# First attention: scores as three products on 64 rows, all engines ordered by pairs of units

## The chip, the cores and the metric

One core of one Trainium2 chip. The metric is the device time of a whole execution in microseconds. The median of three runs of the kernel before is 1353.7 us.

## The reference, cut to what matters

The program is a stack of four blocks on x of 4 x 512 tokens of 256 numbers, each added to x: an attention over a context, a layer of experts, a banded attention over the same context, a second layer of experts. The change touches the first attention alone:

```python
Qh = (queries @ Wq).reshape(n, t, HEADS, D_K)      # queries: layernorm(x), 16 heads of 64
Kh = (keys @ Wk).reshape(n, t, HEADS, D_K)         # keys, values: ctx
Vh = (values @ Wv).reshape(n, t, HEADS, D_V)
energy = jnp.einsum('nqhd,nkhd->nhqk', Qh, Kh) * scale
energy = jnp.where(mask == 0, jnp.asarray(-1e+20, dtype=energy.dtype), energy)
attention = jax.nn.softmax(energy, axis=-1)
heads_out = jnp.einsum('nhqk,nkhd->nqhd', attention, Vh)
return heads_out.reshape(n, t, HEADS * D_V) @ Wo
```

## The kernel before

Numbers that have to be exact are held as a sum of two fp16 tensors, hi and lo (`Split`). A product of two such numbers is three matmuls (`three_products`, L195 to L199): hi hi, hi lo, lo hi.

`phase_attention0` (L235) runs over 4 batches and in each over 8 pairs of heads, 32 groups g in all. A group has 8 units u: two heads a, four tiles qt of 128 queries. Before the change the four tiles of head 0 come first, then those of head 1. A unit goes through five steps. TensorE makes the scores, 128 x 512, into the PSUM bank `sc` (`score`, L419). VectorE adds the mask and takes the maximum (`maximum`, L532, operation L542). ScalarE takes the exponent (`exponent`, L486). TensorE transposes the result in four pieces into `et` (`turn`, L430), ScalarE writes the hi part (`turned_part`, L480) and VectorE the lo part (L516), and TensorE multiplies by v in 12 matmuls of 65 columns (`attend`, L438), the 65th column being the sum of the exponents. After four units of a head VectorE divides (`normalize`, L520).

Each engine runs an order written out by hand. TensorE in turn u does the scores of unit u, the transposes of unit u - 3, the product with v of unit u - 5 (`TURN_LAG`, `ATTEND_LAG`), and then a side job, if there is one. Side jobs (`side_work`, L202) are bound to the unit j within the group: at j = 0 and 1 the projections k and q of the next group, at j = 4 a part of v of the next batch (not in the last batch), at j = 5 in four groups of the second to fourth batch the output projection w of a query tile of the batch before, at j = 7 the transposes t of the outputs of the group before. All side jobs write one of two PSUM banks `pj` in turn, so a job waits until the one two before it has been copied out (`open_group`, L359). The copy is made by ScalarE into `raw` (`copy`, L473), in its turn after that of the job, behind `turned_part` and `exponent` of that turn; for w it is an addition by VectorE. GpSimd then splits `raw` into hi and lo (`split`, L312, operations L333 and L335). `ORDER0` lists all side jobs in order, `GROUP0` and `COPY0` give each its number.

The scores have a contraction over 64 numbers, half of the array's rows. Before the change hi and lo of q are stacked on 128 rows, and k hi twice and k lo twice, by DMA from `nat` (`stack`, L281): so one matmul gives hi hi + lo hi and a second gives hi lo + lo lo (L427, L428). SP's queue issues these eight transfers a group, and behind them the loads of the mask for the next batch.

Of the kernel before, what the change touches and what calls it, by code (L numbers as in the profile page):

```python
# [16 lines left out]
P = 128  # L17
B, S, D = 4, 512, 256
NT = B * S // P
QT = S // P  # L20
# [214 lines left out]
def phase_attention0(nc, sem, T, dram):  # L235
    NBUF = 4
    NRAW = 3
    TURN_LAG, ATTEND_LAG = 3, 5
    with ExitStack() as ctx:
        sb, ps = make_tensors(nc, ctx)  # L240
        v = [Split(sb, f"v{i}", [P, QT, HEADS, VP]) for i in range(2)]
        raw = [sb(f"raw{i}", [P, 512]) for i in range(NRAW)]
        nat = {"q": sb("nat_q", [P, 2, S], F16), "k": sb("nat_k", [P, 2, S], F16)}
        qq = [sb(f"qq{i}", [P, 2, S], F16) for i in range(2)]
        kk = [sb(f"kk{i}", [P, 2, 2, S], F16) for i in range(2)]
        o = [sb(f"o{i}", [P, QT, P]) for i in range(2)]
        o_t = [Split(sb, f"o_t{i}", [P, CT, S]) for i in range(2)]
        masked = [sb(f"masked{i}", [P, S]) for i in range(NBUF)]
# [13 lines left out]
        stacked = [sem(f"stacked{a}") for a in range(2)]  # L262
# [4 lines left out]
        STACKED = 4 * 16  # L267

        def v_part(part, n):
            return part[:, n // 2, (n % 2) * 8:(n % 2 + 1) * 8, 0:DK]  # L270

        with nc.Block() as block:

            @block.sync
            def _(sp):
                def load_mask(n):
                    if n >= 2:
                        sp.wait_ge(bias_ok, n - 1)
                    sp.dma_start(mask_raw[n % 2][:], dram["mask"][n // QT, (n % QT) * P:(n % QT + 1) * P, :]).then_inc(mask_in[n % 2], 16)

                def stack(g):  # L281
                    i = g % 2
                    sp.wait_ge(split_done, COPY0["k", g] + 1)
                    if g >= 2:
                        sp.wait_ge(scores, (g - 1) * UNITS)
                    for a in range(2):
                        for half in range(2):
                            sp.dma_start(kk[i][half * DK:(half + 1) * DK, a, :, :], nat["k"][a * DK:(a + 1) * DK, :, :]).then_inc(stacked[a], 16)
                    sp.wait_ge(split_done, COPY0["q", g] + 1)
                    for a in range(2):  # L290
                        for half in range(2):
                            sp.dma_start(qq[i][half * DK:(half + 1) * DK, a, :], nat["q"][a * DK:(a + 1) * DK, half, :]).then_inc(stacked[a], 16)

                load_mask(0)
                load_mask(1)
                stack(0)
                load_mask(2)
                load_mask(3)
                for g in range(PAIRS0 - 1):
                    stack(g + 1)  # L300
                    if g // PAIRS + 1 < B and g % PAIRS < QT:
                        load_mask((g // PAIRS + 1) * QT + g % PAIRS)

            @block.gpsimd
            def _(pool):
# [52 lines left out]
            def _(pe):  # L358
# [57 lines left out]
                    else:  # L416
                        project_out(what)

                def score(u):  # L419
                    g, j = u // UNITS, u % UNITS  # L420
                    a, qt = j // QT, j % QT
                    if j % QT == 0:
                        pe.wait_ge(stacked[a], STACKED * (g + 1))
                    if u >= 2:
                        pe.wait_ge(masked_ok, u - 1)
                    stat = qq[g % 2][:, a, qt * P:(qt + 1) * P]
                    pe.matmul(sc[j % 2][:], stat, kk[g % 2][:, a, 0, :], start=True, stop=False)  # L427
                    pe.matmul(sc[j % 2][:], stat, kk[g % 2][:, a, 1, :], start=False, stop=True).then_inc(scores, 1)  # L428

                def turn(u):  # L430
                    pe.wait_ge(exp_ok, u + 1)
# [5 lines left out]

                def attend(u):  # L438
                    g, j = u // UNITS, u % UNITS
                    b, a, head = g // PAIRS, j // QT, (g % PAIRS) * 2 + j // QT  # L440
                    if j % QT == 0 and g >= 1:
                        pe.wait_ge(normed, 2 * g - 1 + a)
                    if u % (PAIRS * UNITS) == 0:
                        pe.wait_ge(split_done, COPY0["v", (b, V_GROUPS - 1)] + 1)
                    pe.wait_ge(turned_lo, u + 1)
                    for kt in range(QT):
                        vv = (v[b % 2].hi[:, kt, head, 0:DK + 1], v[b % 2].lo[:, kt, head, 0:DK + 1])
                        mm = three_products(pe, ob[a][:, j % QT, 0:DK + 1], (e_t[u % NBUF].hi[:, kt, :], e_t[u % NBUF].lo[:, kt, :]), vv, kt == 0, kt == QT - 1)
                    mm.then_inc(pv_done, 1)

                project(("k", 0), T.wk0, T.ctx_t)
# [2 lines left out]
                    project_v(("v", (0, n)))  # L454
                pe.wait_ge(v_const, 4)
                units = PAIRS0 * UNITS
                for u in range(units + ATTEND_LAG):
                    if u < units:
                        score(u)
                    if 0 <= u - TURN_LAG < units:  # L460
                        turn(u - TURN_LAG)
                    if u >= ATTEND_LAG:
                        attend(u - ATTEND_LAG)
                    what = side_work(u // UNITS, u % UNITS) if u < units else None
                    if what is not None:
                        do_side_work(what)
# [5 lines left out]
            def _(act):  # L472
# [22 lines left out]
                for n in range(V_GROUPS):  # L495
                    copy(("v", (0, n)))
                units = PAIRS0 * UNITS
                for u in range(units + TURN_LAG):
                    if u >= TURN_LAG:
                        turned_part(u - TURN_LAG)  # L500
                    if u < units:
                        exponent(u)
                    what = side_work((u - 1) // UNITS, (u - 1) % UNITS) if 1 <= u <= units else None
                    if what in COPY0:
                        copy(what)
                copy(("t", PAIRS0 - 1))

            @block.vector
            def _(dve):
# [22 lines left out]
                def maximum(u):  # L532
# [9 lines left out]
                    nc.vector.tensor_tensor_reduce(masked[u % NBUF][:], sc[j % 2][:], mask_bias[g // PAIRS % 2][:, j % QT, :],  # L542
                                                   -SCALE0, 3e38, ALU.add, ALU.min, neg_max[:, g % 2, j:j + 1]).then_inc(masked_ok, 1)

                units = PAIRS0 * UNITS
                for u in range(units + TURN_LAG):
                    if u < units:
                        maximum(u)
                    if u >= TURN_LAG:
                        turned_part(u - TURN_LAG)  # L550
                    if u < units:
                        what = side_work((u - 1) // UNITS, (u - 1) % UNITS) if u >= 1 else None
                        if what in ADD0:
                            add_out(what)
# [1431 lines left out]
```

## Time and profile before

| what | value |
|---|---|
| median of three runs | 1353.7 us (1353.0 to 1359.14) |
| the profiled execution, its own time | 1355.88 us |
| its span | 1354.1 us |
| TensorE busy | 1105.1 us, 82% |
| VectorE busy | 773.4 us, 57% |
| ScalarE busy | 631.1 us, 47% |
| GpSimd busy | 530.1 us, 39% |
| mean granted TensorE clock | 0.908 |

The first attention fills the stretch from about 50 to 577 us. Shares over the span mix stages with different limits, so the stage is read by itself. In the timelines the first column is the start and the second the length, both in us; at the end of a line stands in brackets how long the engine sat idle and what released it. A TensorE matmul is shown with its whole length through the array, so lengths overlap and the distance of two starts is what a matmul takes of the engine. PE is TensorE, DVE VectorE, ACT ScalarE, POOL GpSimd.

### The profile page before, as it was taken

To read this page: it belongs to the slowest core of one execution; us is meant where nothing else is said; L and a number is where in the kernel's file an instruction comes from. 1 tells how busy PE (TensorE), PEld (TensorE's weight loads), DVE (VectorE), ACT (ScalarE), POOL (GpSimd) and SP (SyncE) were. 2 spreads that over 40 slices of the span, in tenths; PEclk is the share of its full clock that TensorE was granted. 3 is DMA by queue.
4 is the path that set the end of the run, shared out by engine and by line. 5 is a ranking of instruction groups with operands and counts; after the bars stand their busy time and mean duration, and the time that the engine had idled before them with its cause. 6 is when DMAs were issued, how large, how long until landed. Compare 5 with 4: busy or idle time off the path is not lost. (4 is left out here: it accounts for less than half of the span.)

```text
span 1354.1 us, 29409 instructions
## 1 busy us (share of the span) xinstructions
PE 1105.1 (82%) x10704; PEld 842.2 (62%) x10705; DVE 773.4 (57%) x2164; ACT 631.1 (47%) x1191; POOL 530.1 (39%) x517
## 2 busy tenths in 40 slices
PE   2399999999999999763999545487899951799996
PEld 1156777777777777562788422355666641688886
DVE  7267787777778778466111062276687651355553
ACT  3277786678668777321222022044455520333331
POOL 2565645545544433190454340588700004011112
PEclk8699999999999999855899859799999975899998
DMA  6222222222222222052365425465422051121110
GB/s 248 54 58 70 53 67 70 57 49 70 68 56 55 48 63 58 1 204 85 107 187 154 89 63 186 127 163 164 127 50 50 18 149 63 33 32 28 26 24 10
DMA packets 80271, 111.08 MB, mean 82 GB/s; under 512 B 11600, under 2 KB 58448, under 8 KB 79760
## 3 DMA queue, kind: packets, MB, share of 16 engines
q1 hardware_dynamic: 69680, 88.30, 22.7%
q0 software_dynamic: 10464, 21.07, 6.7%
q8 instruction: 81, 1.33, 0.4%
q14 instruction: 46, 0.38, 0.1%
HBM read 59.93 MB, written 24.77 MB: 63 GB/s over the span
## 5 line engine op out<-in xcount | busy, mean ns | idle before, releaser
L542 DVE CUSTOM_DVE_ANT_0 masked<-sc,mask_bias 128x512 f32<-128x512 f32 x256 | 175.4, 686 | 58.6 <-issue 39.7
L518 DVE TENSOR_TENSOR e_t_lo<-et,e_t_hi 128x512 f16<-128x512 f32 x256 | 176.6, 690 | 49.8 <-ACT e_t_hi L484 47.4
L491 ACT ACTIVATE e<-masked,neg_max 128x512 f32<-128x512 f32 x256 | 184.0, 719 | 26.6 <-DVE neg_max L542 26.1
L484 ACT ACTIVATE e_t_hi<-et 128x512 f16<-128x512 f32 x256 | 152.0, 594 | 89.5 <-PE et L435 89.0
L435 PEld LDWEIGHTS et<-ident,e 128*128 128x128 f32 x1024 | 125.7, 141 | 54.1 <-ACT e L491 6.1
L435 PE MATMUL et<-ident,e 128*128 128x128 f32 x1024 | 154.2, 273 | 1.4 <-ACT e L491 0.7
L1348 ACT ACTIVATE d_e<-d_st 128x384 f32<-128x384 f32 (+1 forms) x192 | 97.8, 528 | 117.9 <-PE d_st L1433 102.7
L197 PE MATMUL ob<-v_hi,e_t_hi 128*128 128x65 f16 x1024 | 119.1, 193 | 0.6 <-DVE e_t_lo L518 0.6
L198 PE MATMUL ob<-v_lo,e_t_hi 128*128 128x65 f16 x1024 | 119.2, 193 | 0.0
L199 PE MATMUL ob<-v_hi,e_t_lo 128*128 128x65 f16 x1024 | 118.5, 193 | 0.0
L427 PE MATMUL sc<-kk,qq 128*128 128x512 f16 x256 | 97.0, 379 | 6.1 <-DMA qq<-nat_q 5.9
L197 PE MATMUL h_hb<-h_xt_hi,experts_hi 128*128 128x256 f16 x352 | 96.9, 275 | 4.3 <-DVE h_xt_lo L1814 3.9
L1785 POOL DMA_INDIRECT out<-h_res,h_token x22 | 34.3, 1557 | 167.0 <-DVE h_res L1837 161.3
L428 PE MATMUL sc<-kk,qq 128*128 128x512 f16 x256 | 96.9, 379 | 0.0
L198 PE MATMUL h_hb<-h_xt_lo,experts_hi 128*128 128x256 f16 x352 | 96.9, 275 | 0.0
L199 PE MATMUL h_hb<-h_xt_hi,experts_lo 128*128 128x256 f16 x352 | 96.8, 275 | 0.0
L198 PEld LDWEIGHTS ob<-v_lo,e_t_hi 128*128 128x128 f16 x1024 | 94.6, 97 | 2.9
L197 PEld LDWEIGHTS ob<-v_hi,e_t_hi 128*128 128x128 f16 x1024 | 95.7, 97 | 0.8 <-DVE e_t_lo L518 0.7
L199 PEld LDWEIGHTS ob<-v_hi,e_t_lo 128*128 128x128 f16 x1024 | 94.7, 97 | 0.0
L1428 PE MATMUL d_wk<-d_k,d_q 128*128 128x384 f16 (+1 forms) x256 | 71.7, 308 | 23.3 <-DMA d_q<-d_k 20.2
L478 ACT ACTIVATE raw<-pj 128x512 f32<-128x512 f32 x128 | 75.0, 586 | 32.2 <-POOL v_lo L335 16.0
L1360 DVE TENSOR_REDUCE d_mx<-d_wk 128x1 f32<-128x384 f32 x128 | 66.9, 553 | 40.0 <-PE d_wk L1433 33.5
(322 smaller groups left out, 2872.9 us busy)
## 6 DMA issues: line engine op xcount, KB each, us to landing
kk<-nat_k SPq DMA_DIRECT2D x128, 128.0 KB, 2.3
raw<-in_fc SPq DMA_DIRECT2D x16, 1024.0 KB, 6.4
qq<-nat_q SPq DMA_DIRECT2D x128, 64.0 KB, 2.0
mask_raw<-in_mask SPq DMA_DIRECT2D x16, 256.0 KB, 2.9
scratch_stack<-c_qk_hi SPq DMA_DIRECT2D x32, 128.0 KB
scratch_stack<-c_qk_lo SPq DMA_DIRECT2D x32, 128.0 KB
d_expert_raw<-in_gate_w POOLq DMA_DIRECT2D x8, 512.0 KB, 4.3
d_expert_raw<-in_up_w POOLq DMA_DIRECT2D x8, 512.0 KB, 4.0
```

What stands on the lines that cost most here:

```text
L197: pe.matmul(out, stat[0], mov[0], start=first, stop=False)
L198: pe.matmul(out, stat[0], mov[1], start=False, stop=False)
L199: return pe.matmul(out, stat[1], mov[0], start=False, stop=last)
L427: pe.matmul(sc[j % 2][:], stat, kk[g % 2][:, a, 0, :], start=True, stop=False)
L428: pe.matmul(sc[j % 2][:], stat, kk[g % 2][:, a, 1, :], start=False, stop=True).then_inc(scores, 1)
L435: mm = pe.transpose(et[u % 2][:, kt, :], e[u % NBUF][:, kt * P:(kt + 1) * P], T.ident[:])
L478: nc.scalar.activation(raw[n % NRAW][:], pj[GROUP0[what] % 2][:], ACT.Copy).then_inc(copied, 1)
L484: nc.scalar.activation(e_t[u % NBUF].hi[:], et[u % 2][:], ACT.Copy).then_inc(turned_hi, 1)
L491: nc.scalar.activation(e[u % NBUF][:], masked[u % NBUF][:], ACT.Exp, bias=neg_max[:, g % 2, j:j + 1], scale=-1.0).then_inc(exp_ok, 1)
L518: nc.vector.tensor_tensor(e_t[u % NBUF].lo[:], et[u % 2][:], e_t[u % NBUF].hi[:], ALU.subtract).then_inc(turned_lo, 1)
L542: nc.vector.tensor_tensor_reduce(masked[u % NBUF][:], sc[j % 2][:], mask_bias[g // PAIRS % 2][:, j % QT, :], -SCALE0, 3e38, ALU.add, ALU.m ...
L1348: nc.scalar.activation(part(e[m % EBUF][:, 2 * half + i // 3, :, :], i % 3), src, ACT.Exp, scale=SCALE1).then_inc(exp_ok, 1)
```

## The change

Both heads' score of one query tile become one step of TensorE, `score_both`: six matmuls in three rounds, in each round one for head 0 on rows 0 to 63 of the array and one for head 1 on rows 64 to 127, into the two banks `sc`. Their operands are hi and lo of q and k as GpSimd splits them, double buffered; the stacking DMAs, `nat`, `qq`, `kk` and the semaphores for them are gone, and SP's queue holds only mask loads. Units are now ordered by query tile first, head second, and each engine goes on by two units in a turn: TensorE does both scores, both transposes of the pair two back, the side job of the first unit, both products with v of the pair three back, the side job of the second unit. ScalarE does two `turned_part`, two `exponent`, and then the copies of the side jobs of the pair before. VectorE does two maxima, two lo parts, additions, and once in a group both normalizations. The lags become 4 and 6.

```diff
-    TURN_LAG, ATTEND_LAG = 3, 5
+    TURN_LAG, ATTEND_LAG = 4, 6
...
-        nat = {"q": sb("nat_q", [P, 2, S], F16), "k": sb("nat_k", [P, 2, S], F16)}
-        qq = [sb(f"qq{i}", [P, 2, S], F16) for i in range(2)]
-        kk = [sb(f"kk{i}", [P, 2, 2, S], F16) for i in range(2)]
+        heads = {kind: [Split(sb, f"{kind}_heads{i}", [P, S]) for i in range(2)] for kind in ("q", "k")}
...
-                for g in range(PAIRS0 - 1):
-                    stack(g + 1)
-                    if g // PAIRS + 1 < B and g % PAIRS < QT:
-                        load_mask((g // PAIRS + 1) * QT + g % PAIRS)
+                for n in range(NT):
+                    load_mask(n)
...
-                        if at >= 1:
-                            pool.wait_ge(stacked[0], STACKED * at)
-                            pool.wait_ge(stacked[1], STACKED * at)
-                        hi, lo = nat[kind][:, 0, :], nat[kind][:, 1, :]
+                        if at >= 2:
+                            pool.wait_ge(scores, (at - 1) * UNITS)
+                        hi, lo = heads[kind][at % 2].hi[:], heads[kind][at % 2].lo[:]
...
-                def score(u):
...
+                def score_both(u):
+                    g, qt = u // UNITS, u % UNITS // 2
+                    if u % UNITS == 0:
+                        pe.wait_ge(split_done, COPY0["q", g] + 1)
                     if u >= 2:
-                        pe.wait_ge(masked_ok, u - 1)
...
+                        pe.wait_ge(masked_ok, u)
+                    q, k = heads["q"][g % 2], heads["k"][g % 2]
+                    for n, (stat, mov) in enumerate(((q.hi, k.hi), (q.hi, k.lo), (q.lo, k.hi))):
+                        for a in range(2):
+                            rows = slice(a * DK, (a + 1) * DK)
+                            mm = pe.matmul(sc[a][:], stat[rows, qt * P:(qt + 1) * P], mov[rows, :], start=(n == 0), stop=(n == 2))
+                            if n == 2:
+                                mm.then_inc(scores, 1)
...
-                for u in range(units + ATTEND_LAG):
+                for u in range(0, units + ATTEND_LAG, 2):
+                    side = [side_work((u + i) // UNITS, (u + i) % UNITS) if u < units else None for i in range(2)]
                     if u < units:
-                        score(u)
+                        score_both(u)
                     if 0 <= u - TURN_LAG < units:
                         turn(u - TURN_LAG)
+                        turn(u - TURN_LAG + 1)
+                    if side[0] is not None:
+                        do_side_work(side[0])
                     if u >= ATTEND_LAG:
                         attend(u - ATTEND_LAG)
...
+                        attend(u - ATTEND_LAG + 1)
+                    if side[1] is not None:
+                        do_side_work(side[1])
...
-                for u in range(units + TURN_LAG):
+                for u in range(0, units + TURN_LAG, 2):
+                    side = [side_work((u - 2 + i) // UNITS, (u - 2 + i) % UNITS) if 2 <= u <= units else None for i in range(2)]
                     if u >= TURN_LAG:
                         turned_part(u - TURN_LAG)
+                        turned_part(u - TURN_LAG + 1)
                     if u < units:
                         exponent(u)
...
+                        exponent(u + 1)
+                    for what in side:
+                        if what in COPY0:
+                            copy(what)
...
-                    dve.wait_ge(pv_done, g * UNITS + (a + 1) * QT)
+                    dve.wait_ge(pv_done, (g + 1) * UNITS - 1 + a)
...
-                        if u % UNITS == 1 and u >= UNITS:
+                        if u % UNITS == 4 and u >= UNITS:
                             normalize(u // UNITS - 1, 0)
-                        if u % UNITS == 5 and u >= UNITS:
                             normalize(u // UNITS - 1, 1)
```

## Rows read from the trace of the kernel before

**Rows 1.** The page's 40 slices: busy tenths of TensorE.

```profile
PE   2399999999999999763999545487899951799996
```

**Rows 2.** Windows: start, end, length; busy PE, PEld, DVE, ACT, POOL; clock, DMA share, GB/s.

```profile
117.00:549.00 432.00, 428.95 (x5002) 319.93 (x5001) 334.46 (x1043) 326.56 (x565) 206.05 (x224) 1.00 0.24 59
```

**Rows 3.** Waits of 30 to 110 us and of 110 to 549: total, times, longest.

```profile
PE sc L427 <- DMA qq<-nat_q: 2.2, 1, 2.2
...
PE sc L427 <- DMA qq<-nat_q: 3.7, 4, 1.2
```

**Rows 4.** TensorE's timeline, 402.5 to 405.1: start, length, then what ran.

```profile
402.47 0.19 PE L197 MATMUL ob<-v_hi,e_t_hi 128*128 128x65 f16 x1
...
402.83 0.38 PE L197 MATMUL pj<-wv_hi,ctx_t_hi 128*128 128x512 f16 x1
...
404.13 0.38 PE L427 MATMUL sc<-kk,qq 128*128 128x512 f16 x1
404.35 0.38 PE L428 MATMUL sc<-kk,qq 128*128 128x512 f16 x1
404.56 0.60 PE L435 MATMUL et<-ident,e 128*128 128x128 f32 x4
405.00 0.19 PE L197 MATMUL ob<-v_hi,e_t_hi 128*128 128x65 f16 x1
```

**Rows 5.** GpSimd's timeline, 399 to 414: splits of k.

```profile
399.45 0.61 POOL L333 CAST nat_k<-raw 128x512 f16<-128x512 f32 x1 [0.57 <-ACT raw L478]
400.14 1.16 POOL L335 TENSOR_TENSOR nat_k<-raw,nat_k 128x512 f16<-128x512 f32 x1
...
413.63 0.61 POOL L333 CAST nat_k<-raw 128x512 f16<-128x512 f32 x1 [0.21 <-ACT raw L478]
```

**Rows 6.** Groups by line and form: count, busy us, mean ns.

```profile
L427 PE MATMUL sc<-kk,qq 128*128 128x512 f16 x256 | 97.0, 379 | 6.1 <-DMA qq<-nat_q 5.9 <-DVE neg_max L542 0.2
...
L1472 PE MATMUL d_ob<-d_e,v 128*17 128x384 f32 x256 | 23.6, 486 | 0.0
```

**Rows 7.** TensorE's timeline, 908.7 to 911.6, second attention.

```profile
908.79 0.38 PE L1467 MATMUL d_ob<-ident,band 128*128 128x512 bf16 x1
909.10 2.35 PE L1472 MATMUL d_ob<-d_e,v 128*17 128x256 f32 x32
911.38 0.28 PE L1428 MATMUL d_wk<-d_k,d_q 128*128 128x256 f16 x1
```

**Rows 8.** ScalarE's timeline, 404.5 to 407.5.

```profile
405.20 0.60 ACT L484 ACTIVATE e_t_hi<-et 128x512 f16<-128x512 f32 x1 [0.70 <-PE et L435]
405.69 0.71 ACT L491 ACTIVATE e<-masked,neg_max 128x512 f32<-128x512 f32 x1
406.30 0.59 ACT L478 ACTIVATE raw<-pj 128x512 f32<-128x512 f32 x1
406.78 0.60 ACT L484 ACTIVATE e_t_hi<-et 128x512 f16<-128x512 f32 x1
```

**Rows 9.** The timeline of all engines, 66.3 to 67.2.

```profile
66.37 0.60 ACT L478 ACTIVATE raw<-pj 128x512 f32<-128x512 f32 x1 [11.40 <-POOL v_lo L335]
...
67.03 0.61 PE L197 MATMUL pj<-wv_hi,ctx_t_hi 128*128 128x512 f16 x1 [10.53 <-ACT raw L478]
```

**Rows 10.** VectorE's timeline, 404.5 to 407.5.

```profile
404.77 0.69 DVE L542 CUSTOM_DVE_ANT_0 masked<-sc,mask_bias 128x512 f32<-128x512 f32 x1 [0.42 <-issue]
...
405.83 0.69 DVE L518 TENSOR_TENSOR e_t_lo<-et,e_t_hi 128x512 f16<-128x512 f32 x1 [0.36 <-ACT e_t_hi L484]
406.43 0.17 DVE L527 RECIPROCAL rden<-ob 128x4 f32<-128x4 f32 x1
...
406.99 0.69 DVE L542 CUSTOM_DVE_ANT_0 masked<-sc,mask_bias 128x512 f32<-128x512 f32 x1
```

**Rows 11.** The timeline of all engines, 555.0 to 555.9.

```profile
555.05 0.69 DVE L518 TENSOR_TENSOR e_t_lo<-et,e_t_hi 128x512 f16<-128x512 f32 x1 [0.47 <-ACT e_t_hi L484]
...
555.79 0.20 PE L197 MATMUL ob<-v_hi,e_t_hi 128*128 128x65 f16 x1 [0.62 <-DVE e_t_lo L518]
```

More of the change, by code:

```diff
@@ L261, in phase_attention0 @@
         pj_full, copied, added, split_hi, split_done, v_const = (sem(n) for n in ("pj_full", "copied", "added", "split_hi", "split_done", "v_const"))
-        stacked = [sem(f"stacked{a}") for a in range(2)]
         scores, masked_ok, exp_ok = sem("scores"), sem("masked_ok"), sem("exp_ok")
@@ L266, in phase_attention0 @@
         mask_in, bias_ok = [sem(f"mask_in{i}") for i in range(2)], sem("bias_ok")
-        STACKED = 4 * 16
         def v_part(part, n):
@@ L279, in load_mask @@
                     sp.dma_start(mask_raw[n % 2][:], dram["mask"][n // QT, (n % QT) * P:(n % QT + 1) * P, :]).then_inc(mask_in[n % 2], 16)
[L281 to L298, printed above, removed]
-                for g in range(PAIRS0 - 1):
-                    stack(g + 1)
-                    if g // PAIRS + 1 < B and g % PAIRS < QT:
-                        load_mask((g // PAIRS + 1) * QT + g % PAIRS)
+                for n in range(NT):
+                    load_mask(n)
             @block.gpsimd
@@ L417, in do_side_work @@
                         project_out(what)
-                def score(u):
[L420 to L423, printed above, removed]
-                    if u >= 2:
-                        pe.wait_ge(masked_ok, u - 1)
-                    stat = qq[g % 2][:, a, qt * P:(qt + 1) * P]
-                    pe.matmul(sc[j % 2][:], stat, kk[g % 2][:, a, 0, :], start=True, stop=False)
-                    pe.matmul(sc[j % 2][:], stat, kk[g % 2][:, a, 1, :], start=False, stop=True).then_inc(scores, 1)
+                def score_both(u):
+                    g, qt = u // UNITS, u % UNITS // 2
+                    if u % UNITS == 0:
+                        pe.wait_ge(split_done, COPY0["q", g] + 1)
+                    if u >= 2:
+                        pe.wait_ge(masked_ok, u)
[6 more added lines that the diff above has]
+                                mm.then_inc(scores, 1)
                 def turn(u):
@@ L439, in attend @@
                     g, j = u // UNITS, u % UNITS
-                    b, a, head = g // PAIRS, j // QT, (g % PAIRS) * 2 + j // QT
-                    if j % QT == 0 and g >= 1:
+                    b, a, qt, head = g // PAIRS, j % 2, j // 2, (g % PAIRS) * 2 + j % 2
+                    if qt == 0 and g >= 1:
                         pe.wait_ge(normed, 2 * g - 1 + a)
@@ L447, in attend @@
                         vv = (v[b % 2].hi[:, kt, head, 0:DK + 1], v[b % 2].lo[:, kt, head, 0:DK + 1])
-                        mm = three_products(pe, ob[a][:, j % QT, 0:DK + 1], (e_t[u % NBUF].hi[:, kt, :], e_t[u % NBUF].lo[:, kt, :]), vv, kt == 0, kt == QT - 1)
+                        mm = three_products(pe, ob[a][:, qt, 0:DK + 1], (e_t[u % NBUF].hi[:, kt, :], e_t[u % NBUF].lo[:, kt, :]), vv, kt == 0, kt == QT - 1)
                     mm.then_inc(pv_done, 1)
@@ L456, in _ @@
                 units = PAIRS0 * UNITS
-                for u in range(units + ATTEND_LAG):
+                for u in range(0, units + ATTEND_LAG, 2):
+                    side = [side_work((u + i) // UNITS, (u + i) % UNITS) if u < units else None for i in range(2)]
                     if u < units:
-                        score(u)
+                        score_both(u)
                     if 0 <= u - TURN_LAG < units:
                         turn(u - TURN_LAG)
+                        turn(u - TURN_LAG + 1)
+                    if side[0] is not None:
+                        do_side_work(side[0])
                     if u >= ATTEND_LAG:
                         attend(u - ATTEND_LAG)
-                    what = side_work(u // UNITS, u % UNITS) if u < units else None
-                    if what is not None:
-                        do_side_work(what)
+                        attend(u - ATTEND_LAG + 1)
+                    if side[1] is not None:
+                        do_side_work(side[1])
                 turn_out(("t", PAIRS0 - 1))
@@ L497, in _ @@
                 units = PAIRS0 * UNITS
-                for u in range(units + TURN_LAG):
+                for u in range(0, units + TURN_LAG, 2):
+                    side = [side_work((u - 2 + i) // UNITS, (u - 2 + i) % UNITS) if 2 <= u <= units else None for i in range(2)]
                     if u >= TURN_LAG:
                         turned_part(u - TURN_LAG)
+                        turned_part(u - TURN_LAG + 1)
                     if u < units:
                         exponent(u)
-                    what = side_work((u - 1) // UNITS, (u - 1) % UNITS) if 1 <= u <= units else None
-                    if what in COPY0:
-                        copy(what)
+                        exponent(u + 1)
+                    for what in side:
+                        if what in COPY0:
+                            copy(what)
                 copy(("t", PAIRS0 - 1))
@@ L540, in maximum @@
                     nc.vector.memset(gate[:, u % (2 * UNITS):u % (2 * UNITS) + 1], 0.0)
-                    nc.vector.tensor_tensor_reduce(masked[u % NBUF][:], sc[j % 2][:], mask_bias[g // PAIRS % 2][:, j % QT, :],
+                    nc.vector.tensor_tensor_reduce(masked[u % NBUF][:], sc[j % 2][:], mask_bias[g // PAIRS % 2][:, j // 2, :],
                                                    -SCALE0, 3e38, ALU.add, ALU.min, neg_max[:, g % 2, j:j + 1]).then_inc(masked_ok, 1)
                 units = PAIRS0 * UNITS
-                for u in range(units + TURN_LAG):
+                for u in range(0, units + TURN_LAG, 2):
                     if u < units:
                         maximum(u)
+                        maximum(u + 1)
                     if u >= TURN_LAG:
                         turned_part(u - TURN_LAG)
+                        turned_part(u - TURN_LAG + 1)
                     if u < units:
-                        what = side_work((u - 1) // UNITS, (u - 1) % UNITS) if u >= 1 else None
-                        if what in ADD0:
-                            add_out(what)
-                        if u % UNITS == 1 and u >= UNITS:
+                        for i in range(2):
+                            what = side_work((u - 2 + i) // UNITS, (u - 2 + i) % UNITS) if u >= 2 else None
+                            if what in ADD0:
+                                add_out(what)
+                        if u % UNITS == 4 and u >= UNITS:
                             normalize(u // UNITS - 1, 0)
-                        if u % UNITS == 5 and u >= UNITS:
                             normalize(u // UNITS - 1, 1)
```

## The prediction

> **What bounds the kernel now.** I read the busy slices of the page first. From about 70 us to 540 us TensorE is at nine tenths or more in every slice [rows 1]. That stretch is the first attention. The table by windows says the same in numbers: in 432 us TensorE is busy 428.95, VectorE 334.46, ScalarE 326.56 and GpSimd 206.05, at a granted clock of 1.00 [rows 2]. So the sum of what TensorE has to do sets the pace, and two engines stand at three quarters. The list of waits then tells what the remaining TensorE idle time is: in the loop it waited for the stacking DMAs of `qq` 3.7 us in four waits, and 2.2 us once at its beginning [rows 3]. There is no wait of TensorE for a projection bank copied out by ScalarE in that loop.
>
> The TensorE timeline gives the pieces as distances between starts, which is what counts on a pipelined engine [rows 4]. A projection of six 512-column matmuls takes 404.13 - 402.83 = 1.30 us, one score matmul 0.216 (404.35 - 404.13), so the two of a unit 0.43; the four transposes 0.44 (404.56 to 405.00); the twelve products of one unit with v 0.36 (402.47 to 402.83). A group of eight units is 8 x 1.23 = 9.86 plus k, q, v at 1.30 and four transposes of o at 0.44: 14.2 us. The split of k recurs after 413.63 - 399.45 = 14.18 us [rows 5], so the pieces are complete. Nothing but TensorE is in this period.
>
> **The change, part by part.**
>
> *Products.* For two units, four matmuls of 0.216 (0.864 us) become six of 64 rows. If the two heads of a round run side by side, three rounds take 0.648, a saving of 0.216. No 64-row matmul is in this trace. The nearest thing is the product with v of the second attention, which puts four heads on separate columns of the array: 256 matmuls of 384 columns lasting 486 ns each, 124 us if one followed the other, fill only 23.6 us of busy time, where 256 full-size score matmuls of 379 ns fill 97.0, all of their length [rows 6]. So matmuls on disjoint parts of the array do run at once here. These are columns, not rows, but it is the nearest row and I take it. The same place prices the way in and out. The full-size 512-column matmul at 908.79 should free the array at +0.216; the packed ones start at 909.10, 0.31 later, so entry costs 0.09. The 32 packed ones are 16 of 256 columns and 16 of 384; at the 0.108 us for 128 fp32 columns of [rows 4] one quarter of them takes 4 x 0.216 + 4 x 0.324 = 2.16, and the next full-size matmul starts 911.38 - 909.10 = 2.28 after: exit costs 0.12 [rows 7]. With 0.21 for the round trip, a pair of units costs 0.648 + 0.21 = 0.858 against 0.864. Over 128 pairs: **-0.8 us**. Bounds: 0.216 x 128 = 27.6 us of gain if there is no such cost, and 0.648 x 128 = 83 us of loss with the six serial.
>
> The Trainium skill speaks against the change here: TensorEngine Tiling, Key Properties, says that changing the tiling mode drains TensorE. The 0.09 and 0.12 of this trace agree with that rule. TensorE: Matmul & The Clock Gate, Part 3, gives a packed group the length of one matmul plus about 4 ns per further tile and names no price for entering; by it alone the sum would have the full gain of 27.6 us, which is a rival below.
>
> *The stacking DMAs go.* 256 transfers leave SP's queue, and the mask loads behind them come earlier. TensorE gets the two waits of [rows 3] back: **-5.9 us**. GpSimd now splits k and q straight into the operands; its k and q splits are as many as before, and the q split is done before the next group's first scores (from the times below: k is there at 1.81 and q at 2.29 of the third pair, a split takes 0.69 + 1.16 [rows 5], so both are ready at 5.5; the scores start at 6.8, in the last batch without w at 5.4, which I count as met).
>
> *The order by pairs, and what now queues behind what.* This is the part that costs. A projection bank `pj` is one of two, so each TensorE side job waits until ScalarE has copied the job two before it. ScalarE copies the side jobs of pair i only in its turn i+1, behind two `turned_part` and two `exponent` of that turn, and `turned_part` waits for TensorE's transposes of the same turn. In the old order the copy stood one unit later, behind one of each. From the start of a pair's scores I lay out both engines. TensorE: scores 0.65, exit 0.12, eight transposes (0.87) from 0.77 to 1.64, first side job, v products 0.73 (what two units of 1.23 leave), second side job, entry 0.09. ScalarE: it starts 0.64 after the transposes start (404.56 to 405.20 [rows 4, 8]), so at 1.41; two e_t copies of 0.49, two exponents of 0.61, so a projection copy starts at 3.61 [rows 8]; and a second copy at 4.09 (0.48 on); TensorE goes on 0.66 after a copy starts (66.37 to 67.03 [rows 9]), at 4.27. The maxima don't delay the exponents: they start 0.42 after the last score matmul starts (404.35 to 404.77 [rows 4, 10]), at 0.86, and are 0.60 apart. Behind the waiting matmul stands all of TensorE's queue, and VectorE and ScalarE hang on it.
> - q of the next group, last in the first pair, needs the copy of the turned o (`t`), which is copied in this same pair. TensorE reaches it at 1.64 + 1.30 + 0.73 = 3.67 and may go at 4.27: 0.60 us, in groups 2 to 30, 29 times: **+17.4 us**.
> - v, in the third pair, needs k, copied in the second. The second pair has no side job and lasts 0.65 + 0.12 + 0.87 + 0.73 + 0.09 = 2.46; k is free at 4.27 - 2.46 = 1.81 of the third, v is reached at 1.64: 0.17, 23 times: **+3.9 us**.
> - t, last in the fourth pair, stands two behind v in the groups that also have a `w`. It is reached at 1.64 + 0.73 = 2.37 and may go at 4.27: 1.90 us. These are four groups in each of the second and third batch, 8: **+15.2 us**.
>
> *Both normalizations in one turn.* Each takes 0.56 of VectorE (406.43 to 406.99 [rows 10]), and its product with v must be ready, so both follow the third pair's e_t work. With v or w in that pair TensorE is slower than that, and they cost nothing. In the last batch without w (groups 24, 29, 30) ScalarE comes 0.7 late from two copies, VectorE ends its e_t work at 3.96 and the two at 5.08, the next maxima at 2.62 and 3.23 of the fourth pair; TensorE may start scores 0.74 after the second one starts (as an e_t operation at 555.05 lets it go at 555.79 [rows 11]), at 3.97, and wants to at 2.9. 1.1 us, 3 times: **+3.3 us**. `masked_ok` is now awaited for both units of the last pair rather than for the one before last; in the second pair it is met at 1.46 + 0.74 = 2.20 against 2.46. That margin of 0.26 is what hides it; gone, each 0.1 us costs 13 us over all pairs.
>
> *Ends.* One unit more of lag at the tail and two normalizations behind each other: between -1 and +2, taken as **+0.5 us**. Later stages are untouched.
>
> Sum: -0.8 - 5.9 + 17.4 + 3.9 + 15.2 + 3.3 + 0.5 = +33.6 us. The profiled execution took 1355.88 us (span 1354.1), so 1389.5 in its terms; it was 2.2 above the median of the runs. Against the median of 1353.7 it is 1387.3.
>
> **Rivals.**
> - *Entering and leaving is free or hidden.* For it: on row halves the weights of one half could be loaded while the other runs. Against it: the two gaps of [rows 7]. The waits for copies stay, since both sides of them move together. 1387.3 - 0.21 x 128 = 1360.4.
> - *The copy waits don't arise*, because ScalarE reaches the copies sooner than laid out. For it: ScalarE is busy only three quarters. Against: its wait is one of order, not load. Then 1387.3 - 36.5 = 1350.8.
> - *Faster than before:* both of these. The packed rounds then pay from the first pair of units on, and this decides once a copied bank is open less than 3.67 us after the pair's scores start. 1387.3 - 26.9 - 36.5 = 1323.9.
> - *The heads don't run side by side*, so that the change doesn't do what it says: what packs in [rows 6] is columns. Six serial rounds add 0.648 x 128 = 83 us: 1470.
> - A round trip half as dear again as 0.21, since here two full sets of 128 weight columns go in where [rows 7] has 17, would add 13 us: 1400. I hold it within the forecast.
>
> **How the numbers follow.** Forecast 0.62, free entry 0.15, no copy waits 0.08, both 0.07, not side by side 0.08. The likeliest gives 1387. The range reaches down to 1349, past the case without copy waits and past free entry, and up to 1402 for the dearer round trip; it leaves out the 0.15 of the last two cases and some 0.05 in the tails. A measurement tells about 0.5% from no change, that is 1347 to 1360.5. Faster: the 0.07 and 0.03 of the case at 1350.8, 0.10. Same: the rest of that case and half of the one at 1360.4, 0.13. Slower: 0.77.
>
> **What would show it.** In the profile after: 64-row score matmuls with two starting within some ns and rounds 0.216 apart (side by side), about 0.09 ahead of and 0.12 behind each six (the drain); TensorE waiting for `raw` before q some 29 times by 0.6, and some 8 times by 1.9 before the turned o; no DMA wait before scores; the group period about 14.9 us where it was 14.2. It is wrong if ScalarE's waits end earlier, if the rounds are 0.43 apart, or if the maxima end later than laid out, so that scores wait for VectorE in most pairs.

## The result and the profile after

The changed kernel takes 1386.28 us, the median of four runs, against 1355.15 for the kernel before measured beside it: a ratio of 1.0236, 95% interval 1.0201 to 1.0271. The forecast was 1387, slower. The profiled execution took 1386.59 us with a span of 1384.9.

First the window of the first attention after (columns as in [rows 2]):

The changed kernel, windows:

```profile
110.00:565.00 455.00, 428.60 (x5030) 286.94 (x5027) 308.11 (x998) 299.25 (x543) 197.07 (x216) 1.00 0.02 6
```


TensorE, which had 3 us without work in 432 [rows 2], now has 26.4 in 455. VectorE and ScalarE have no more work than before (760.3 and 616.3 us over the whole kernel, against 773.4 and 631.1) and more idle time. The waits of TensorE's matmuls in that loop name it; at the end of a line stand the total in us, how many waits, and the longest (the other engines' waits, and those of TensorE's weight loads, are left out):

The changed kernel, waits:

```profile
...
PE pj L368 <- ACT raw L459: 13.7, 8, 1.7
PE pj L197 <- ACT raw L459: 11.5, 27, 0.4
...
PE sc L403 <- DVE neg_max L526: 1.0, 3, 0.3
```


The two DMA waits of [rows 3] are gone and TensorE waits for `raw`, the copied-out projection banks. In time, this is the first pair of one group (start, length, what ran):

The changed kernel, TensorE's timeline:

```profile
394.26 0.39 PE L403 MATMUL sc<-k_heads_hi,q_heads_hi 64*128 64x512 f16 x2
...
397.93 0.19 PE L199 MATMUL ob<-v_hi,e_t_lo 128*128 128x65 f16 x1
398.55 0.39 PE L197 MATMUL pj<-z_t_hi,wq_hi 128*128 128x512 f16 x1 [0.43 <-ACT raw L459]
...
399.64 0.38 PE L199 MATMUL pj<-z_t_hi,wq_lo 128*128 128x512 f16 x1
399.95 0.39 PE L403 MATMUL sc<-k_heads_hi,q_heads_hi 64*128 64x512 f16 x2
400.18 0.38 PE L403 MATMUL sc<-k_heads_lo,q_heads_hi 64*128 64x512 f16 x2
400.39 0.38 PE L403 MATMUL sc<-k_heads_hi,q_heads_lo 64*128 64x512 f16 x2
400.70 1.09 PE L412 MATMUL et<-ident,e 128*128 128x128 f32 x8
```

The changed kernel, ScalarE's timeline:

```profile
395.70 1.09 ACT L465 ACTIVATE e_t_hi<-et 128x512 f16<-128x512 f32 x2 [2.09 <-PE et L412]
396.68 1.33 ACT L472 ACTIVATE e<-masked,neg_max 128x512 f32<-128x512 f32 x2
397.90 0.59 ACT L459 ACTIVATE raw<-pj 128x512 f32<-128x512 f32 x1
```


This pair's scores started at 394.26. TensorE reached q at 397.93 + 0.03 = 397.96 and ran it at 398.55, 0.59 later. ScalarE's copy before it started at 397.90, behind two e_t copies and two exponents, and 0.65 after its start TensorE went on: these are the pieces of [rows 8] and [rows 9] in another order. The same rows hold the packed scores, to be set beside [rows 4] and [rows 7]. The two matmuls of a round are one row of two, rounds are 0.21 to 0.23 apart; the first starts 399.95 - 399.64 = 0.31 after the last full-size matmul, which needs 0.216, and the transposes start 0.31 after the last round.

Where the 30.8 us of span went, by the first and last score matmul and the first matmul of the stage behind (72.3 and 549.1 before, where the last one is that of L428 behind the 548.9 of the row shown; 65.5 and 577.3 after):

The changed kernel, matmuls of one line:

```profile
L403 PE MATMUL sc<-k_heads_hi,q_heads_hi x256: 372/387/388, 65.5 to 576.9; 64*128 64x512 f16 x128
...
L403 PE MATMUL sc<-k_heads_hi,q_heads_lo x256: 374/376/377, 66.0 to 577.3; 64*128 64x512 f16 x128
```

The kernel before, matmuls of one line:

```profile
L427 PE MATMUL sc<-kk,qq x256: 375/379/391, 72.3 to 548.9; 128*128 128x512 f16 x128
```

The kernel before, TensorE's timeline:

```profile
579.37 0.88 PE L739 MATMUL r_tb<-ident,r_xf 128*128 128x128 f32 x3 [6.17 <-DVE r_xf L810]
```

The changed kernel, TensorE's timeline:

```profile
609.82 1.09 PE L725 MATMUL r_tb<-ident,r_xf 128*128 128x128 f32 x4 [6.17 <-DVE r_xf L796]
```


The loop is 35.0 us longer (511.8 against 476.8), it begins 6.8 earlier, of which 0.7 is the head of the kernel and 6.1 are this stage's, the tail is 2.2 us longer (609.8 - 577.3 = 32.5 against 30.3), and the stages behind are 0.3 longer.

### The profile page after: what moved, and what is told of

The parts are those of the page before. It is cut to its first block and busy times, and to the rows that moved or that the text cites. A ratio compares the mean times of both kernels' runs of the same rounds, so it can differ in the third digit from the quotient of the medians.

```text
span 1384.9 us, 29599 instructions
## 1 busy us (share of the span) xinstructions
PE 1122.7 (81%) x10960; PEld 818.6 (59%) x10961; DVE 760.3 (55%) x2164; ACT 616.3 (45%) x1191; POOL 529.8 (38%) x517
## 5 line engine op out<-in xcount | busy, mean ns | idle before, releaser
L465 ACT ACTIVATE e_t_hi<-et 128x512 f16<-128x512 f32 x256 | 140.0, 601 | 165.7 <-PE et L412 165.6
L502 DVE TENSOR_TENSOR e_t_lo<-et,e_t_hi 128x512 f16<-128x512 f32 x256 | 164.6, 684 | 18.9 <-ACT e_t_hi L465 18.7
L472 ACT ACTIVATE e<-masked,neg_max 128x512 f32<-128x512 f32 x256 | 171.6, 729 | 2.3 <-DVE neg_max L526 2.3
L412 PEld LDWEIGHTS et<-ident,e 128*128 128x128 f32 x1024 | 110.0, 141 | 56.6 <-issue 33.4
L412 PE MATMUL et<-ident,e 128*128 128x128 f32 x1024 | 141.2, 281 | 1.9 <-DVE e_t_lo L502 1.0
L197 PE MATMUL ob<-v_hi,e_t_hi 128*128 128x65 f16 x1024 | 106.5, 193 | 0.2
L198 PE MATMUL ob<-v_lo,e_t_hi 128*128 128x65 f16 x1024 | 106.5, 193 | 0.0
L199 PE MATMUL ob<-v_hi,e_t_lo 128*128 128x65 f16 x1024 | 106.0, 193 | 0.0
L1414 PE MATMUL d_st<-d_q,d_k 128*128 128x384 f16 (+1 forms) x256 | 70.9, 305 | 13.7 <-DMA d_q<-d_shift 12.8
L1787 ACT ACTIVATE h_silu<-h_hb 128x256 f32<-128x256 f32 x88 | 33.7, 383 | 107.0 <-PE h_hb L199 107.0
```

The source lines that it names most:

```text
L197: pe.matmul(out, stat[0], mov[0], start=first, stop=False)
L198: pe.matmul(out, stat[0], mov[1], start=False, stop=False)
L199: return pe.matmul(out, stat[1], mov[0], start=False, stop=last)
L412: mm = pe.transpose(et[u % 2][:, kt, :], e[u % NBUF][:, kt * P:(kt + 1) * P], T.ident[:])
L465: nc.scalar.activation(e_t[u % NBUF].hi[:], et[u % 2][:], ACT.Copy).then_inc(turned_hi, 1)
L472: nc.scalar.activation(e[u % NBUF][:], masked[u % NBUF][:], ACT.Exp, bias=neg_max[:, g % 2, j:j + 1], scale=-1.0).then_inc(exp_ok, 1)
```

## The experiments

All compare with the kernel before measured beside them, whose median was 1355.3 us (1355.5 for the same rows and the two excursions). The stages behind this one, which no edit here touches, take 771 to 779 us from one trace to the next, so the loop from the first to the last score matmul is the finer measure and is given where it decides.

### Copies first

```diff
                     side = [side_work((u - 2 + i) // UNITS, (u - 2 + i) % UNITS) if 2 <= u <= units else None for i in range(2)]
+                    for what in side:
+                        if what in COPY0:
+                            copy(what)
                     if u >= TURN_LAG:
                         turned_part(u - TURN_LAG)
...
                         exponent(u + 1)
-                    for what in side:
-                        if what in COPY0:
-                            copy(what)
```

> The changed kernel, with one thing moved: ScalarE makes the copies of the side jobs of the pair before at the head of its turn, ahead of turned_part and exponent. Theory A (the loss is a wait of order): the three waits of TensorE for raw in the trace after (16.5 us before q, 15.0 before the turned o, 2.5 before v, by distances between starts) go, 1386.3 - 34.0 = 1352 us, a plain group lasts 14.35 instead of 15.07 us. Rival B (ScalarE or VectorE is too slow for pairs, and the wait only shows at pj): the waits come back at the transposes or the scores and the time stays above 1375. Rival C (the loss is mostly the way in and out of the 64-row form): the time stays above 1370 too, but no wait for raw is left.

Measured: 1345.4 us, ratio to the kernel before 0.9927 (0.9902 to 0.9952), so 41 us less than the changed kernel, where 34 were expected. In the loop TensorE is busy 426 of 427 us and has no wait for `raw` left:

Copies first, windows:

```profile
110.00:537.00 427.00, 426.03 (x5157) 291.56 (x5155) 316.52 (x1027) 313.62 (x557) 200.30 (x219) 1.00 0.02 6
```

Copies first, waits:

```profile
ACT raw L459 <- PE pj L199: 26.9, 28, 1.0
...
PE sc L403 <- DVE neg_max L526: 1.0, 3, 0.3
```

Copies first, matmuls of one line:

```profile
L403 PE MATMUL sc<-k_heads_hi,q_heads_hi x256: 372/387/388, 66.3 to 539.3; 64*128 64x512 f16 x128
...
L403 PE MATMUL sc<-k_heads_hi,q_heads_lo x256: 374/376/376, 66.7 to 539.8; 64*128 64x512 f16 x128
```


The wait has turned round: ScalarE waits for the bank (26.9 us), which costs nothing. The loop lasts 473.5, that is 38.3 less, where 34 were expected from the waits for `raw`; of the difference 1.7 us is in the last batch and 1.7 in one stretch at half clock (both below), and 0.9 is spread over the groups. The other 2.6 us of the 41 lie in the spread of the runs, which go from 1341.3 to 1351.4. Theory A holds, B and C fall. A group without w recurs, by its k split (start and length on GpSimd), after 191.69 - 176.62 = 15.07 us in the changed kernel and after 182.35 - 167.99 = 14.36 here:

The changed kernel, GpSimd's timeline:

```profile
176.62 0.61 POOL L307 CAST k_heads_hi<-raw 128x512 f16<-128x512 f32 x1 [3.85 <-ACT raw L459]
...
191.69 0.61 POOL L307 CAST k_heads_hi<-raw 128x512 f16<-128x512 f32 x1 [3.85 <-ACT raw L459]
```

Copies first, GpSimd's timeline:

```profile
167.99 0.61 POOL L307 CAST k_heads_hi<-raw 128x512 f16<-128x512 f32 x1 [1.12 <-ACT raw L459]
...
182.35 0.61 POOL L307 CAST k_heads_hi<-raw 128x512 f16<-128x512 f32 x1 [1.12 <-ACT raw L459]
```


### Four full-size matmuls for the packed six, with either order of copies

```diff
-                    for n, (stat, mov) in enumerate(((q.hi, k.hi), (q.hi, k.lo), (q.lo, k.hi))):
+                    for n, (stat, mov) in enumerate(((q.hi, k.hi), (q.lo, k.lo))):
                         for a in range(2):
-                            rows = slice(a * DK, (a + 1) * DK)
-                            mm = pe.matmul(sc[a][:], stat[rows, qt * P:(qt + 1) * P], mov[rows, :], start=(n == 0), stop=(n == 2))
+                            mm = pe.matmul(sc[a][:], stat[:, qt * P:(qt + 1) * P], mov[:, :], start=(n == 0), stop=(n == 1))
-                            if n == 2:
+                            if n == 1:
```

The scores are then sums over both heads and lack one product; the run is there for its time alone.

> The changed kernel with four matmuls on all 128 rows in place of the six on 64 (so the scores are sums over both heads, and one of the three products is left out), nothing else touched. It prices the packed six against four full ones in the order by pairs. Theory A (the array pays about 0.25 us for each excursion, 0.648 + 0.253 = 0.901 against 0.864): 0.037 x 128 = 4.8 us faster than the changed kernel, 1381.5. Rival D (the excursion is free and only looks dear in the trace, the packing saves 0.216 a pair): 27.6 us slower, 1414.

> Both edits: copies at the head of ScalarE's turn and four full-row matmuls (scores over both heads, one product left out). This is the order by pairs without stacking DMAs, without the 64-row form and without the order's wait. If the two costs are independent, 1352 - 4.8 = 1347 us. If the packing is worth 27.6 us, 1380. If the order by pairs costs anything beyond the copies, it is above 1350 with both gone.

Measured: 1379.96 us with the order of the change (1.0174, 1.0147 to 1.0201) and 1341.14 with copies first (0.9900, 0.9871 to 0.9929). The full-size form is faster than the packed one by 6.3 and by 4.3 us, where the excursion's price (the way of the array into the 64-row form and back) gave 4.8. The intervals of the second pair overlap, so the time alone does not show this small a difference; the traces do: with copies first the loop lasts 469.0 against 473.5 us, and a plain group 14.20 against 14.36, 0.04 for each of its four pairs. Rival D, for which 27.6 us in the other direction were expected, falls: packing three rounds into the array's halves is worth slightly less than nothing here. With both costs gone a group takes 180.35 - 166.15 = 14.20 us, the period of the kernel before, so in a plain group the order by pairs costs nothing beyond the copies and the packing.:

Full-size four, copies first, GpSimd's timeline:

```profile
166.15 0.61 POOL L307 CAST k_heads_hi<-raw 128x512 f16<-128x512 f32 x1 [1.08 <-ACT raw L458]
...
180.35 0.61 POOL L307 CAST k_heads_hi<-raw 128x512 f16<-128x512 f32 x1 [1.08 <-ACT raw L458]
```

In the last batch something is left: its groups without v or w last 13.41 us, where the kernel before has 13.05 and 13.12. TensorE waits 0.39 there for the maxima that follow both normalizations.

### Both matmuls of a round on the same rows

This one and the next have the copies first, too. The second head's scores are left out here.

```diff
-                            rows = slice(a * DK, (a + 1) * DK)
+                            rows = slice(0, DK)
```

> The kernel with the copies first, and in it both matmuls of each round on rows 0 to 63 (the scores of the second head are then those of the first, so its part of the computation is left out). The 64-row form, its entry and its exit stay, side by side is impossible. Theory A (two matmuls on different rows run at once, which saves a whole 0.216 us a round): 3 x 0.216 x 128 = 83 us slower than with the copies first, 1345.4 + 83 = 1428 us. Rival G (the two starts 3 ns apart in the trace are only how they are recorded, and the array takes them one after the other in part): less than 40 us slower, below 1385.

Measured: 1429.78 us (1.0550, 1.0531 to 1.0569), 84.4 more than with the copies first; expected 83. The loop lasts 556.2 us, 82.7 more. By form, the score matmuls of one product, after and here (count, busy us, mean ns):

The changed kernel, groups by form:

```profile
L403 PE MATMUL sc<-k_heads_lo,q_heads_hi 64*128 64x512 f16 x256 | 48.6, 376 | 0.0
```

Same rows, groups by form:

```profile
L403 PE MATMUL sc<-k_heads_lo,q_heads_hi 64*128 64x512 f16 x256 | 75.8, 376 | 0.0
```

Same rows, TensorE's timeline:

```profile
301.05 0.60 PE L403 MATMUL sc<-k_heads_hi,q_heads_hi 64*128 64x512 f16 x2
301.49 0.59 PE L403 MATMUL sc<-k_heads_lo,q_heads_hi 64*128 64x512 f16 x2
301.93 0.59 PE L403 MATMUL sc<-k_heads_hi,q_heads_lo 64*128 64x512 f16 x2
302.45 1.09 PE L412 MATMUL et<-ident,e 128*128 128x128 f32 x8
```


256 matmuls of the same 376 ns fill 48.6 us side by side and 75.8 on the same rows (lengths still overlap there), and the rounds are 0.44 apart instead of 0.21 to 0.23. The two heads do run at once; rival G falls.

### Two excursions in each pair

The third round moves behind the first of the pair's transposes; inside `score_both`:

```diff
...
+                    rounds(slice(0, 2))
+                    between()
+                    rounds(slice(2, 3))
...
-                        score_both(u)
+                        score_both(u, (lambda: turn(u - TURN_LAG, (0,))) if u >= TURN_LAG else (lambda: None))
                     if 0 <= u - TURN_LAG < units:
-                        turn(u - TURN_LAG)
+                        turn(u - TURN_LAG, (1, 2, 3) if u < units else range(QT))
```

> The kernel with the copies first, and in it the third round of each pair's scores after the first of the eight transposes, so that the array goes into the 64-row form and out of it twice a pair. Same matmuls, same result. Theory A (0.25 us for each excursion): 0.253 x 128 = 32 us slower, 1345.4 + 32 = 1378 us, a plain group lasts 15.4 instead of 14.36 us. Rival D (the excursion is nearly free): within 5 us of 1345.4. Rival H (the scores are late for VectorE by the same edit and that dominates): slower by over 45 us, with TensorE waiting for neg_max in most pairs.

Measured: 1382.0 us (1.0182, 1.0146 to 1.0219), 36.6 more than with the copies first. The loop itself grew by 32.2 us, as expected by 32 (first to last score matmul, 505.6 against 473.5); the rest lies in the spread of the runs, whose four times go from 1376.6 to 1385.9. The splits of k of two plain groups start at 175.26 and 190.64, so a group takes 15.38 us, 1.02 more for four more excursions. In one pair both can be read:

Two excursions, TensorE's timeline:

```profile
301.27 0.38 PE L404 MATMUL sc<-k_heads_lo,q_heads_hi 64*128 64x512 f16 x2
301.58 0.33 PE L418 MATMUL et<-ident,e 128*128 128x128 f32 x1
301.84 0.39 PE L404 MATMUL sc<-k_heads_hi,q_heads_lo 64*128 64x512 f16 x2
302.16 0.98 PE L418 MATMUL et<-ident,e 128*128 128x128 f32 x7
```


The round at 301.27 frees the array at 301.49, the transpose starts at 301.58, 0.09 late; it needs 0.109, the next round starts 0.26 after it, 0.15 late. Rivals D and H fall.

### The kernel before with its mask loads first

```diff
                 load_mask(1)
+                load_mask(2)
+                load_mask(3)
                 stack(0)
-                load_mask(2)
-                load_mask(3)
                 for g in range(PAIRS0 - 1):
-                    stack(g + 1)
                     if g // PAIRS + 1 < B and g % PAIRS < QT:
                         load_mask((g // PAIRS + 1) * QT + g % PAIRS)
+                    stack(g + 1)
```

> The kernel before with SP's queue reordered alone: each mask load stands ahead of the stacking DMAs beside it, at the start and in the loop. The trace after has its first scores 6.1 us earlier, counted from the first transposes, which the prediction did not have. Theory E (GpSimd waited for mask loads that stood behind the stacking DMAs, 10 us in four waits at most, and split v late): 6 us faster at the start, and the waits of the first groups for qq go in part, up to 4 us more: 1345 to 1349 against 1355.2. Rival F (the start gained because GpSimd no longer waits for the stacked tensors): no change, 1355.

Measured: 1344.13 us (0.9924, 0.9897 to 0.9951), 11 less than the kernel before, with all stacking DMAs in place; 1345 to 1349 were expected. The first scores start at 65.3 and the loop is 4.3 us shorter (first to last score matmul):

The kernel before, masks first, matmuls of one line:

```profile
L427 PE MATMUL sc<-kk,qq x256: 376/379/390, 65.3 to 537.6; 128*128 128x512 f16 x128
```

The kernel before, GpSimd's timeline:

```profile
53.13 1.15 POOL L335 TENSOR_TENSOR nat_q<-raw,nat_q 128x512 f16<-128x512 f32 x1
60.69 3.83 POOL L310 TENSOR_SCALAR mask_bias<-mask_raw 128x512 bf16<-128x512 int32 x2 [6.41 <-DMA mask_raw<-in_mask]
64.47 0.61 POOL L333 CAST v_hi<-raw 128x512 f16<-128x512 f32 x1
```

The changed kernel, GpSimd's timeline:

```profile
52.40 1.15 POOL L309 TENSOR_TENSOR q_heads_lo<-raw,q_heads_hi 128x512 f16<-128x512 f32 x1
53.52 3.83 POOL L285 TENSOR_SCALAR mask_bias<-mask_raw 128x512 bf16<-128x512 int32 x2
57.30 0.61 POOL L307 CAST v_hi<-raw 128x512 f16<-128x512 f32 x1
```


The last six rows are GpSimd's. In the kernel before it ended the split of q at 54.3 and stood until 60.69, 6.41 us, for a mask that SP had queued behind the stacking DMAs of group 0, which themselves waited for that split; only then did it split v, ScalarE's ring `raw` filled and TensorE waited for its banks. (From 30 to 110 us GpSimd waited 21.8 us for masks in four waits, twice what the expectation says.) In the changed kernel the mask work follows at once. Theory E holds, F falls.

The loop gained, too, because TensorE's waits for `qq` after 110 us, 3.7 us in [rows 3], are gone with the stacking DMAs still there. One wait is left, at the beginning of the loop:

The kernel before, masks first, waits of 30 to 110 us:

```profile
PE sc L427 <- DMA qq<-nat_q: 1.9, 1, 1.9
```

So those 3.7 us came from where the mask loads stood in SP's queue, and only the wait at the beginning stays with the stacking.

## Why the prediction was right

The sign and the mechanism of the loss came out as forecast: TensorE waits for copies that ScalarE makes too late in its order. That the time came out within 1 us of the forecast (33.6 us on 1353.7 forecast, 31.1 on 1355.15 measured) is luck in part, for two terms were wrong by about 6 us each and nearly cancel: the packed scores (forecast -0.8, measured +5) and the start of the stage (no price, measured -6.1). Point by point, with waits as distances between starts, summed over the matmuls of the loop (the DMA row is what is left of the 35 us when the other rows of the loop are taken off):

| step | forecast, us | measured, us |
|---|---|---|
| q waits for the copy of t | +17.4 | +16.5 (28 x 0.59, from the third group on but for the one at half clock) |
| t waits for the copy of v | +15.2 | +15.0 (8 x 1.88) |
| v waits for the copy of k | +3.9 | +2.5 (24 x 0.107) |
| both normalizations, last batch | +3.3 | +3.1 (3 x 1.03) |
| six packed for four full | -0.8 | +5 |
| stacking DMAs gone, loop | -5.9 | about -8.5, with a shorter first group |
| half clock once | none | +1.7 |
| ends | +0.5 | +2 |
| start of the stage | none | -6.1 |

The waits. The period of a plain group was forecast at about 14.9 us and is 15.07. TensorE's arrival at q was laid out at 3.67 after the pair's scores and its release at 4.27; the trace has 3.70 (394.26 to 397.96) and 4.29. The longest wait, before the turned o in a group with w and v:

The changed kernel, TensorE's timeline:

```profile
411.36 0.19 PE L199 MATMUL ob<-v_hi,e_t_lo 128*128 128x65 f16 x1
413.27 0.66 PE L368 MATMUL pj<-ident,o 128*128 128x128 f32 x4 [1.72 <-ACT raw L459]
```

The changed kernel, ScalarE's timeline:

```profile
410.43 1.08 ACT L465 ACTIVATE e_t_hi<-et 128x512 f16<-128x512 f32 x2 [3.57 <-PE et L412]
411.40 1.33 ACT L472 ACTIVATE e<-masked,neg_max 128x512 f32<-128x512 f32 x2
412.62 0.59 ACT L459 ACTIVATE raw<-pj 128x512 f32<-128x512 f32 x1
```


411.36 + 0.03 to 413.27 is 1.88 us, and the copy that releases it starts at 412.62, last in ScalarE's turn. Moving the copies alone to the head of the turn took these waits away, and 38.3 us of loop with them, so their cause is shown, not argued.

The packing. The step that was mis-sized is the round trip of 0.21 from [rows 7]. By the trace's nanoseconds (medians of the distances between starts, less what the matmul itself takes) entry takes 0.096, the first round 0.010 more than the others and the exit 0.091: that is about the 0.21 of there. The rest, 0.056, is the first transpose after the exit, which takes 0.165 us where the others take 0.109: eight of them last 1.09 in the trace after, where four more on the 0.60 of [rows 4] would make 1.04. In [rows 7] the matmul behind the exit is fp16, and I took nothing for an fp32 one. The 0.056 does not belong to the exit alone: with four full-size matmuls, where no 64-row one runs, the first transpose behind the scores takes 0.109 like the others, but the first behind each of the eight waits of 1.88 us takes 0.165 as well. So the excursion costs 0.25, as the two excursions showed by doubling it, the six come to 0.901 against 0.864, and 0.037 x 128 = 4.8; the full-size four gave 6.3 and 4.3. The Trainium skill (TensorEngine Tiling, Key Properties) says that changing the tiling mode drains TensorE; the 0.096 in and the 0.091 out agree with it. The Trainium skill (TensorE: Matmul & The Clock Gate, Part 3) gives a packed group the length of one matmul plus about 4 ns per further tile; for the part between entry and exit the trace agrees, with the two starts of a round 3 ns apart in the median.

Of the rivals, the free entry fell with the two excursions, the heads one after the other with the same rows, and both cases without copy waits with the trace after.

The stacking DMAs. The measured -8.5 is a rest and not a measurement of its own. What the prediction put down to the transfers being gone was for the most part where the mask loads stood behind them: with the masks first the kernel before got 4.3 us of its loop back with every transfer in place.

The start was overlooked. I read TensorE's DMA waits in the loop and not GpSimd's before it, so moving mask loads out from behind the stacking DMAs was put at "come earlier" with no price. It is worth 6 us, and the kernel before with the new queue order, whose first scores come as early (65.3 us), showed that it is this and nothing else of the change.

The last batch. Some 1.0 us a group came where 1.1 was forecast, but not where I put it: 0.33 and 0.13 lie before transposes, 0.18 between products and 0.39 before scores, since ScalarE's lateness reaches VectorE's e_t work and through it the `et` banks too. That the size came out is luck. With the copies first only the 0.39 is left.

The changed kernel, TensorE's timeline:

```profile
471.93 1.22 PE L412 MATMUL et<-ident,e 128*128 128x128 f32 x8 [0.26 <-DVE e_t_lo L502]
...
474.86 0.39 PE L403 MATMUL sc<-k_heads_hi,q_heads_hi 64*128 64x512 f16 x2 [0.33 <-DVE neg_max L526]
```


The clock. Not foreseen: behind a wait of 1.88 us (the one that ends at 413.27) TensorE ran one stretch at 1.2 GHz. Windows of that place (columns as in [rows 2]), and the transposes of that pair:

The changed kernel, windows:

```profile
409.00:413.00 4.00, 2.55 (x39) 1.88 (x38) 2.85 (x9) 2.57 (x5) 0.00 (x0) 1.00 0.00 0
415.00:418.00 3.00, 3.00 (x12) 1.83 (x11) 2.42 (x7) 2.19 (x4) 0.08 (x1) 0.50 0.00 0
```

The changed kernel, TensorE's timeline:

```profile
414.61 1.76 PE L412 MATMUL et<-ident,e 128*128 128x128 f32 x8
```


These transposes took 1.76 us instead of 1.09. It happened behind one of the eight waits of that length and made the group that follows last 16.16 where its like have 15.07: 1.7 for the clock, less the 0.59 of q, which did not have to wait there. With four full-size matmuls and the order of the change there are eight waits of 1.88 us too, and the granted clock stays at 1.00 behind all of them. In the run with both matmuls on the same rows it stood at 0.50 from 75.1 to 78.5 us, behind a wait of 1.20 us for the maxima. Why behind these only stays open.

## What to carry to other kernels

Where an engine waits for a buffer of two, lay out in time from a common event where the copy stands in the copying engine's order and where the waiter arrives: coarser turns move the copy back although no engine has more to do, and here that alone was 34 us of waits that moving three lines gave back. Price the way into and out of a divided array against what one packed group saves (0.25 against 0.22 us here; a longer packed group could pay, which no run here tried). When transfers leave a queue, look at what stood behind them on every engine from the stage's first microsecond on: that gain is had in the kernel before by reordering SP's queue, 1344.13 us. The changed kernel at its best, with the copies first, takes 1345.4, so packing and order by pairs together show no gain over the old order with its masks first.

## What was new about the hardware

- Two matmuls on different halves of the array's rows, into different PSUM banks, run fully at once: rounds of 0.216 us for both (first round 0.226), 0.44 when both use the same rows.
- Going from full-size matmuls to 64-row ones and back costs 0.25 us in all: 0.096 in, 0.010 on the first round, 0.091 out, 0.056 on the first fp32 transpose behind. The last of these comes behind a wait of 1.88 us as well, without any 64-row matmul.
- Once in sixteen waits of 1.88 us inside otherwise dense work (eight in the changed kernel, eight with four full-size matmuls) the granted clock fell behind it: it stood at 0.50 from 415 to 418 us, and each transpose there took twice the time (0.213 us instead of 0.109).
